# Edge counts of a graph attention layer: sorted into buckets and counted behind the projection, instead of counted one tile at a time ahead of it

## The chip, the cores and the metric

The kernel runs on one core of a Trainium2 chip, in one launch. The metric is the device time in microseconds (us) of that core. Five engines work in parallel, each through its own list of instructions, and meet at semaphores: TensorE (PE, matmuls, writes PSUM; PEld is its weight load), VectorE (DVE), ScalarE (ACT), GpSimd (POOL) and SyncE (SP, which issues the DMAs).

## The reference

```python
xn = layernorm(x)                                      # x: 625 x 1024
z  = einsum('ni,hif->nhf', xn, W)                      # 4 heads of 256: 625 x 1024
el, er = (z * a_l).sum(-1), (z * a_r).sum(-1)
e  = leaky_relu(el[src] + er[dst], 0.2)                # 10000 edges
ex = exp(e - segment_max(e, dst)[dst])
gnn = segment_sum(ex / segment_sum(ex, dst)[dst] * z[src], dst)
q, k, v = split(xn @ w_qkv); q, k = elu(q) + 1, elu(k) + 1       # 16 heads of 64
mix = (q @ (k.T @ v)) / (q @ k.sum()) @ w_o
x = x + gnn + mix
out = x + ternary_ffn(layernorm(x)) + bias             # int8 rounded input, ternary weights
```

An edge (src, dst) enters the attention only through its pair. So the kernel needs one 625 x 625 table, how many edges go from each source to each target; with it, the edge softmax becomes a dense one with the exponentials multiplied by `counts`, and with `no_edge`, a mask where the count is zero.

## The kernel before

The 625 nodes are five tiles (NT) of 125 rows (P), the 1024 features eight blocks of 128 (KT). Projections go in chunks of 512 columns: z is Z_CH = 2 chunks, then KV_CH = 4 chunks of k and v, then q, the output product and the ternary layer. A float32 product is three passes, high by high, low by high, high by low (`three_pass`, L988 to L990); ScalarE makes the high part of each weight unit (`hi_unit`, L344), GpSimd the low part (`lo_quad`, L304), four units ahead of TensorE. A `step` is one weight unit against all five row tiles, 15 matmuls of 512 columns.

Before z the edges are counted. They are 80 columns of 125 edges. For each column VectorE (`onehots`, L586 and L588) writes a one-hot of the targets, 125 x 626 in bf16, and one of the sources by pairs, 125 x 314, whose value is 1 for an even source and 4096 for an odd one. TensorE (`edge_tiles`, L1015) multiplies them, five matmuls a column, one for each tile of 125 targets, and adds up in PSUM banks 0 to 4. The 80 columns are three groups (GROUP_SEGS), so that no sum passes 4096; after each ScalarE copies the banks (`copy_counts`, L371). Between the columns VectorE does the layer norm of each row tile in steps (`statistics`), ScalarE scales the rows (`row`, L352, L355), TensorE transposes them (`row_transposes`, L1004), and ScalarE and GpSimd split them into `act_hi` and `act_lo`. ScalarE also takes the absolute sums of the ternary weights there (`abs_of`, L377).

When the last group is copied, TensorE begins z (L988, the loop over `step(c, k, ...)`), and VectorE unpacks the three packed sums into `counts` and `no_edge` (L636 to L660). VectorE's list then goes on with `take_z(0)` (`junk` L678, the products with a_l and a_r, and `z_lo` L684), the ternary scale, the diagonals (L693), `take_z(1)` and the scores. Two waits tie the engines here:

```python
act.wait_ge(z_used, c * NT + (nt + 1))        # ScalarE, ahead of each copy of z out of PSUM (L417)
dve.sem_inc(z_used, NT)                       # VectorE, behind no_edge
pe.wait_ge(bank_free, (ci + NG - 1) * NT + (nt + 1))   # TensorE, ahead of a chunk's first step
```

The next loop (j = 0, 1) runs k and v with the GAT units between the steps: in step 1 `el` is spread over the partitions (L1092), and from step 5 on (UNIT_STEPS) each unit transposes `prob` (L1078), which VectorE makes from the scores (L732), ScalarE's exponentials and `counts` (L751, L753). Everything behind it is the same in both kernels.

## Time and profile before

| | us |
|---|---|
| median of 3 runs | 469.44 (467.74 to 470.69) |
| the profiled execution, its own time | 471.35 |
| its span, first to last instruction | 469.6 |
| TensorE busy | 446.0 |
| VectorE busy | 345.0 |
| ScalarE busy | 190.5 |
| GpSimd busy | 138.4 |

The busy time of an engine is an average over stages with different limits: it tells who is full, not who is waited for. A window gives the same numbers for one stage. The chain that ended last goes back from the last instruction, at each step to what released it. A row of the timeline has the start, the length, the engine, the line in the kernel, and the tile written <- the tiles read. The granted clock is TensorE's, as a share of 2.4 GHz.

### The profile page before, as it was taken

To read this page: it belongs to the slowest core of one execution; us is meant where nothing else is said; L and a number is where in the kernel's file an instruction comes from. 1 tells how busy PE (TensorE), PEld (TensorE's weight loads), DVE (VectorE), ACT (ScalarE), POOL (GpSimd) and SP (SyncE) were. 2 spreads that over 40 slices of the span, in tenths; PEclk is the share of its full clock that TensorE was granted. 3 is DMA by queue.
4 is the path that set the end of the run, shared out by engine and by line. 5 is a ranking of instruction groups with operands and counts; after the bars stand their busy time and mean duration, and the time that the engine had idled before them with its cause. 6 is when DMAs were issued, how large, how long until landed. Compare 5 with 4: busy or idle time off the path is not lost.

```text
span 469.6 us, 8351 instructions
## 1 busy us (share of the span) xinstructions
PE 446.0 (95%) x2707; PEld 384.2 (82%) x2707; DVE 345.0 (73%) x905; ACT 190.5 (41%) x337; POOL 138.4 (29%) x105
## 2 busy tenths in 40 slices
PE   7799999989999899999999999999999999989897
PEld 4699898768787787779888788799999888868665
DVE  5999997998569778984157799636556468798773
ACT  2476562125173475445245544425433122212162
POOL 2421133544331422122232321247776000051200
PEclk9989999999999999999999999999999999998999
DMA  8833240322221311111121111136663011020024
GB/s 206 241 91 91 89 136 1 90 67 67 67 67 47 89 47 45 46 45 47 45 67 45 45 45 45 45 93 198 183 188 105 22 46 45 7 82 1 1 87 132
DMA packets 19207, 36.47 MB, mean 78 GB/s; under 512 B 2593, under 2 KB 2843, under 8 KB 19054
## 3 DMA queue, kind: packets, MB, share of 16 engines
q1 hardware_dynamic: 19179, 36.11, 26.6%
q8 instruction: 16, 0.26, 0.2%
q14 instruction: 12, 0.10, 0.1%
HBM read 33.54 MB, written 2.56 MB: 77 GB/s over the span
## 4 chain that ended last, share of the span: by engine, by line
PE 63%; DVE 22%; issue 7%; ACT 3%; DMA 2%; SPq 1%; DVEq 1%; ACTq 0%
PE ps L988 14%; PE ps L989 14%; PE ps L990 14%; PE ps L1015 9%; PE ps L1243 4%; DMA w_raw<-in_weights 2%; PE ps L1078 2%; DVE exp_a L751 2%; DVE score L732 2%; PE ps L1130 2%; DVE junk L678 1%; DVE k_sb L721 1%; DVE packed L642 1%; PE ps L1113 1%; DVE unpack L639 1%
## 5 line engine op out<-in xcount | busy, mean ns | idle before, releaser
L304 POOL TENSOR_TENSOR w_lo<-w_raw,w_hi 128x512 fp32r<-128x512 f32 x52 | 73.4, 1416 | 179.7 <-ACT w_hi L344 179.7
L988 PE MATMUL ps<-w_hi,act_hi 128*125 128x512 f32 x240 | 96.8, 403 | 2.3 <-ACT tmp L417 2.2
L989 PE MATMUL ps<-w_lo,act_hi 128*125 128x512 f32 x240 | 94.6, 394 | 0.0
L990 PE MATMUL ps<-w_hi,act_lo 128*125 128x512 f32 x240 | 94.5, 394 | 0.0
L1015 PE MATMUL ps<-onehot_src,onehot_dst 125*125 125x314 bf16 x400 | 60.2, 310 | 5.0 <-DVE onehot_src L588 4.9
L1015 PEld LDWEIGHTS ps<-onehot_src,onehot_dst 125*125 125x125 bf16 x400 | 54.9, 143 | 9.8 <-DVE onehot_src L588 5.8
L344 ACT ACTIVATE w_hi<-w_raw 128x512 fp32r<-128x512 f32 x52 | 32.8, 633 | 73.0 <-PE ps L990 70.9
L988 PEld LDWEIGHTS ps<-w_hi,act_hi 128*125 128x125 f32 x240 | 44.5, 185 | 12.8 <-ACT tmp L417 2.6
L990 PEld LDWEIGHTS ps<-w_hi,act_lo 128*125 128x125 f32 x240 | 44.5, 185 | 11.3
L989 PEld LDWEIGHTS ps<-w_lo,act_hi 128*125 128x125 f32 x240 | 44.5, 185 | 9.9
L988 PE MATMUL ps<-act_hi,w_hi 128*128 128x312 f32 (+1 forms) x128 | 39.7, 310 | 0.0
L989 PE MATMUL ps<-act_lo,w_hi 128*128 128x312 f32 (+1 forms) x128 | 39.1, 306 | 0.0
L990 PE MATMUL ps<-act_hi,w_lo 128*128 128x312 f32 (+1 forms) x128 | 39.1, 306 | 0.0
L588 DVE TENSOR_SCALAR onehot_src<-iota,src_half,src_worth 125x314 bf16<-125x314 f16 x80 | 35.8, 447 | 0.0
L988 PE MATMUL ps<-wo_hi,act_hi 128*125 128x512 f32 (+1 forms) x88 | 34.3, 389 | 0.0
L989 PE MATMUL ps<-wo_lo,act_hi 128*125 128x512 f32 (+1 forms) x88 | 33.4, 380 | 0.0
L990 PE MATMUL ps<-wo_hi,act_lo 128*125 128x512 f32 (+1 forms) x88 | 33.2, 377 | 0.0
L586 DVE TENSOR_SCALAR onehot_dst<-iota,dst_f 125x626 bf16<-125x626 f16 x80 | 32.4, 405 | 0.9 <-DVE bn L599 0.4
L337 POOL TENSOR_TENSOR x_sb<-x_sb,bias_sb 125x1024 f32<-125x1024 f32 x5 | 11.8, 2371 | 67.8 <-DMA bias_sb<-in_bias 50.9
L456 ACT ACTIVATE pt_hi<-ps 125x625 fp32r<-125x625 f32 x20 | 13.9, 693 | 36.1 <-PE ps L1078 36.1
L988 PE MATMUL ps<-z_hi,pt_hi 125*125 x100 | 28.1, 281 | 0.0
L989 PE MATMUL ps<-z_lo,pt_hi 125*125 x100 | 28.0, 280 | 0.0
(151 smaller groups left out, 878.6 us busy)
## 6 DMA issues: line engine op xcount, KB each, us to landing
w_raw<-in_weights SPq DMA_DIRECT2D x80, 256.0 KB, 2.7
f_raw<-in_ffn_weights SPq DMA_DIRECT2D x32, 256.0 KB, 2.9
x_sb<-in_x SPq DMA_DIRECT2D x5, 448.0 KB
out<-x_sb SPq DMA_DIRECT2D x9, 224.0 KB
alr<-in_a_lr SPq DMA_DIRECT2D x1, 896.0 KB
bias_sb<-in_bias SPq DMA_DIRECT2D x1, 448.0 KB
x_sb<-in_x SPq DMA_DIRECT2D x5, 52.0 KB
out<-x_sb SPq DMA_DIRECT2D x9, 26.0 KB
```

The lines of the kernel that those rows point to most:

```text
L304: pool.tensor_tensor(w_lo[:, s, :], w_raw[:, s, :], w_hi[:, s, :].bitcast(f32), ALU.subtract).then_inc(w_ready, 1)
L337: pool.tensor_tensor(x_sb[:, t, :], x_sb[:, t, :], bias_sb[:], ALU.add).then_inc(biased, 1)
L344: act.activation(w_hi[:, slot, :], w_raw[:, slot, :], ACT.Copy).then_inc(w_hi_ready, 1)
L456: act.activation(pt_hi[:], pt_ps[:P, 0:NT, :P], ACT.Copy).then_inc(pt_hi_ready, 1)
L586: dve.tensor_scalar(onehot_dst[:, s % RING, :], iota[:], dst_f[:, ds(n * SEG + s, 1)], None, ALU.is_equal).then_inc(oh_ready, 1)
L588: dve.tensor_scalar(onehot_src[:, s % RING, :], iota[:, :HALF], src_half[:, ds(n * SEG + s, 1)], src_worth[:, ds(n * SEG + s, 1)], ALU.is_ ...
L732: dve.tensor_tensor_reduce(out=score[:, u % 2, :], in0=no_edge[:, dt, :N], in1=el_rows[:, a, :], scale=1.0, scalar=2 * NEG, op0=ALU.add, o ...
L988: pe.matmul(dst, a[0], b[0], start=first, stop=False)
L989: pe.matmul(dst, a[0], b[1], start=False, stop=False)
L990: return pe.matmul(dst, a[1], b[0], start=False, stop=last)
L1015: last = pe.matmul(ps[:P, nt, :HALF], onehot_dst[:, s, nt * P:(nt + 1) * P], onehot_src[:, s, :], start=opens and s == 0, stop=False)
L1243: last = pe.matmul(ps[:P, part_bank(t, i), :hi - lo], quant_t[:, t % 2, k, :P], tern[:, k, lo:hi], start=k == 0, stop=k == KT - 1)
```

## The change

The edges are no longer counted ahead of z. They are sorted on the chip first, and counted behind z.

A bucket is one tile of 125 targets by a third of the sources (SPART = 209): 5 x 3 = 15 buckets. VectorE works out each edge's bucket (`buckets`), the running count in each bucket by a scan, and, with the totals of the rows by two small matmuls (L1166, L1167), its place (`places`). Each bucket gets whole units of 256 places, 54 units in all, that is 108 tiles of 128 slots. Ten `route` batches move the edges' codes to their places: VectorE writes one-hots of the place's partition (`route_p`) and column (`route_c`, multiplied by the code), TensorE multiplies eight columns of edges a batch (L1152) into bank 7. `decode` takes target and source back out of the code. Then 14 batches of `count_onehots` (108 tiles in eights, the last a half) give a one-hot of 125 targets and one of 209 sources, and TensorE needs one matmul of 209 columns for a tile, where it needed five of 314 for a column of edges. Which PSUM columns a unit adds to depends on its bucket: `unit_columns` writes the addresses, and TensorE loads them into registers, four at a time (`load_units`, TENSOR_LOAD, L1157). The one-hots are f16 with four tiles innermost, so TensorE reads them with a stride of four elements.

The order: `buckets` stands ahead of the layer norm; the row tiles' low halves are now VectorE's (`split_lo`) and not GpSimd's; `abs_of` moves into z's first half on ScalarE, with the DMAs of the ternary weights on SyncE between those of z's weights; route batches 0 to 7 stand behind steps 4 to 7 of z's first half, 8 and 9 behind step 0 of its second; the counting stands behind z. New waits: TensorE's matmul for the ternary scale waits for `fscale` and `slots`, its clearing of bank 7 waits for the scale (`fscale`, 2), ScalarE's `z_hi` waits for the last route batch, the j loop's first step waits for `count_out` (five copies of the counts), VectorE's `no_edge` for all eight.

```diff
+    SPART = (N + 2) // 3
+    NB = NT * 3
+    UT = 2
+    USLOTS = UT * 128
+    UNITS = (E + NB * (USLOTS - 1)) // USLOTS
+    TILES = UNITS * UT
+    ULOAD = 4
+    UPAD = (UNITS + ULOAD - 1) // ULOAD * ULOAD
+    BATCH = 8
+    NROUTE = ET // BATCH
+    NOH = (TILES + BATCH - 1) // BATCH
+    RSLOTS = 4
+    OHSLOTS = 7
+    CODE0 = 1024
...
+            for k in range(KT - 1):
+
+                sp.wait_ge(w_ready, k + 1)
+                sp.dma_start(w_raw[:, k % QUAD, :], weights[QUAD + k]).then_inc(raw_in[k % QUAD], 16)
+                for s in range(2):
+                    sp.wait_ge(f_abs, 2 * k + s + 1)
+                    sp.dma_start(f_raw[:, s, :], ffn_weights[2 * k + 2 + s]).then_inc(f_in[s], 16)
+            sp.wait_ge(w_ready, KT)
+            sp.dma_start(w_raw[:, QUAD - 1, :], weights[QUAD + KT - 1]).then_inc(raw_in[QUAD - 1], 16)
+            with sp.Fori(KT // QUAD + 1, QA) as q:
...
+                    act.activation(act_hi[:, 4 * b:4 * b + 4, t * P:(t + 1) * P], row_ps(t, b),
+                                   ACT.Copy).then_inc(act_hi_in, 1)
+
+            def abs_of(u):
+
+                act.wait_ge(f_in[u % 2], 16 * (u // 2 + 1))
+                act.activation(f_raw[:, u % 2, :], f_raw[:, u % 2, :], ACT.Abs,
+                               accum_out=abs_sum[:, u:u + 1]).then_inc(f_abs, 1)
...
-            with act.Fori(0, Z_CH) as c:
+            for c in range(Z_CH):
                 for k in range(KT - 1):
                     step_split(c, k, c * 2 + (k // QUAD + 1))
+                    if c == 0:
+                        abs_of(2 * k)
+                        abs_of(2 * k + 1)
                 for nt in range(NT):
                     act.wait_ge(proj_done, c * NT + (nt + 1))
 
                     act.wait_ge(z_used, c * NT + (nt + 1))
                     act.activation(tmp[:, nt, :], ps[:P, nt, :], ACT.Copy).then_inc(bank_free, 1)
                 step_split(c, KT - 1, c * 2 + 2)
+                if c == 0:
+                    abs_of(NU - 2)
+                    abs_of(NU - 1)
+                    act.wait_ge(route_used, NROUTE)
                 for nt in range(NT):
-                    act.wait_ge(bank_free, (c + NG) * NT + (nt + 1))
-                    act.activation(z_hi[:, nt, ds(c * CH, CH)], tmp[:, nt, :], ACT.Copy).then_inc(z_hi_ready, 1)
+                    act.wait_ge(bank_free, c * NT + (nt + 1))
+                    act.activation(z_hi[:, nt, c * CH:(c + 1) * CH], tmp[:, nt, :], ACT.Copy).then_inc(z_hi_ready, 1)
+
+
+            act.wait_ge(count_done, 8)
...
+                dve.tensor_tensor(member.rearrange("p (b e) -> p b e", e=ET), bucket_iota[:],
+                                  edge_c.rearrange("p (o e) -> p o e", o=1).broadcast_to([P, NB, ET]),
+                                  ALU.is_equal).then_inc(edge, 1)
+                dve.wait_ge(edge, 10)
+
+                dve.tensor_tensor_scan(upto[:, 1:], member[:], member[:], 0.0, ALU.add, ALU.max).then_inc(edge, 1)
+                dve.wait_ge(edge, 11)
+                dve.tensor_tensor(row_tot[:], upto[:, ET::ET], upto[:, 0:NB * ET:ET], ALU.subtract).then_inc(masks, 1)
...
+            def route_onehots(i):
+
+                slot = i % RSLOTS
+                if i >= RSLOTS:
+                    dve.wait_ge(route_used, i - RSLOTS + 1)
+
+                def of(t, n):
+                    return t[:, BATCH * i:BATCH * (i + 1)].rearrange("p (g o t) -> p g o t", o=1, t=4).broadcast_to([P, 2, n, 4])
+
+                def counted(n):
+                    return count_iota[:P, :n, :].rearrange("p (o n) t -> p o n t", o=1).broadcast_to([P, 2, n, 4])
+
+                dve.tensor_tensor(route_p[:, slot], counted(128), of(edge_p, 128), ALU.is_equal).then_inc(routes, 1)
+                dve.tensor_tensor(route_c[:, slot], counted(TILES), of(edge_c, TILES), ALU.is_equal).then_inc(routes, 1)
+                dve.wait_ge(routes, 3 * i + 2)
+                dve.tensor_tensor(route_c[:, slot], route_c[:, slot], of(edge_v.bitcast(f16), TILES), ALU.mult).then_inc(routes, 1)
...
+            def count_onehots(i):
...
+                dve.tensor_tensor(onehot_d[slot][:, :g], counted(P), of(slot_d, P), ALU.is_equal).then_inc(oh_ready, 1)
+                dve.tensor_tensor(onehot_s[slot][:, :g], counted(SPART), of(slot_s, SPART), ALU.is_equal).then_inc(oh_ready, 1)
...
+            buckets()
+            statistics(0)
+            statistics(1)
+            root(0)
+            statistics(2)
+            root(1)
+            split_lo(0)
+            for t in range(1, NT):
+                if t + 2 < NT:
+                    statistics(t + 2)
+                if t + 1 < NT:
+                    root(t + 1)
+                split_lo(t)
+            codes()
+            places()
+            unit_columns()
             dve.wait_ge(row_t, 2 * NT)
-
-
-            ups = 0
-            dve.wait_ge(bank_free, NG * NT)
-            for g in range(NG):
-                pk, un, cs = packed[:, g, :, :], unpack[:], csum[:]
-                dve.tensor_scalar(un, pk, -BASE / 2.0 + 48.0, 1.0 / BASE, ALU.add, ALU.mult).then_inc(up, 1)
-                ups += 1
-                dve.wait_ge(up, ups)
-                dve.tensor_scalar(un, un, MAGIC, MAGIC, ALU.add, ALU.subtract).then_inc(up, 1)
-                ups += 1
-                dve.wait_ge(up, ups)
-                dve.scalar_tensor_tensor(pk, un, -float(BASE), pk, ALU.mult, ALU.add).then_inc(up, 1)
-                if g == 0:
-                    dve.tensor_copy(cs, un).then_inc(up, 1)
-                elif g < NG - 1:
-                    dve.tensor_tensor(cs, cs, un, ALU.add).then_inc(up, 1)
-                else:
-                    dve.tensor_tensor(counts[:, :, 1:NPAD:2], cs[:, :, :NPAD // 2], un[:, :, :NPAD // 2],
-                                      ALU.add).then_inc(up, 1)
-                ups += 2
-                dve.wait_ge(up, ups)
-            for g in range(1, NG - 1):
-                dve.tensor_tensor(packed[:, 0, :, :], packed[:, 0, :, :], packed[:, g, :, :], ALU.add).then_inc(up, 1)
-                ups += 1
-                dve.wait_ge(up, ups)
-            dve.tensor_tensor(counts[:, :, 0:NPAD:2], packed[:, 0, :, :NPAD // 2],
-                              packed[:, NG - 1, :, :NPAD // 2], ALU.add).then_inc(up, 1)
-            ups += 1
-            dve.wait_ge(up, ups)
-            dve.tensor_scalar(no_edge[:], counts[:], 0.0, NEG, ALU.is_equal, ALU.mult).then_inc(up, 1)
-            ups += 1
-            dve.wait_ge(up, ups)
             dve.sem_inc(z_used, NT)
-
-
-            dve.wait_ge(alr_in, 2 * 16)
-            dve.sem_inc(el, 1)
+            dve.wait_ge(edge, 15)
+            for i in range(NROUTE):
+                route_onehots(i)
+            decode()
...
+            OH_A = OHSLOTS // 2
+            for i in range(OH_A):
+                count_onehots(i)
+            dve.wait_ge(alr_in, 2 * 16)
+            dve.sem_inc(el, 1)
             take_z(0)
-
-            dve.wait_ge(fs_ps, 1)
-            dve.tensor_scalar(scales[:, 0:1], ps[:, 7, 0:1], 1.0 / (D * D), None, ALU.mult).then_inc(fscale, 1)
+            dve.wait_ge(f_abs, NU)
+            dve.reduce_sum(abs_sum[:, NU:NU + 1], abs_sum[:, :NU], axis=AX.X).then_inc(fscale, 1)
+            for i in range(OH_A, OHSLOTS):
+                count_onehots(i)
+            scale_of()
             diagonals(0)
-            dve.wait_ge(fscale, 2)
-            dve.tensor_scalar(scales[:, 1:2], scales[:, 0:1], 0.5, None, ALU.mult).then_inc(fscale, 1)
-            dve.tensor_scalar(scales[:, 2:3], scales[:, 0:1], -0.5, None, ALU.mult).then_inc(fscale, 1)
-            dve.wait_ge(fscale, 4)
+            for i in range(OHSLOTS, NOH):
+                count_onehots(i)
             take_z(1)
             dve.wait_ge(z_used, (1 + Z_CH) * NT)
             diagonals(1)
+            dve.wait_ge(count_out, 8)
+            dve.tensor_scalar(no_edge[:], counts[:], 0.0, NEG, ALU.is_equal, ALU.mult).then_inc(up, 1)
...
+            for k in range(KT):
+                step(0, k, k + 1, k % QUAD)
+                if k >= 4:
+                    route(2 * (k - 4))
+                    route(2 * (k - 4) + 1)
+
+            unit_at = []
+            for k in range(KT):
+                step(1, k, KT + k + 1, k % QUAD)
+                if k == 0:
+                    route(NROUTE - 2)
+                    route(NROUTE - 1)
+                    pe.wait_ge(cols_ready, 1)
+                elif k == KT - 2:
+                    pe.wait_ge(fscale, 1)
+                    pe.wait_ge(slots, 1)
+                    pe.matmul(ps[:, 7, 0:1], ones[:], abs_sum[:, NU:NU + 1], start=True, stop=True).then_inc(fs_ps, 1)
+                unit_at += load_units(k)
+
+            flat = ps[:P].rearrange("p b n -> p (b n)")
+            for b in (5, 6, 7, 0, 1, 2, 3, 4):
+                if b == 7:
+                    pe.wait_ge(fscale, 2)
+                elif b < NT:
+                    pe.wait_ge(bank_free, NT + b + 1)
+                pe.matmul(ps[:P, b, :2 * SPART], zeros[:, :P], zeros[:, :2 * SPART], start=True, stop=False)
+            for u in range(UNITS):
+                if u % ULOAD == 0 and u // ULOAD >= KT:
+                    unit_at += load_units(u // ULOAD)
+                for i in range(u * UT, (u + 1) * UT):
+                    if i % BATCH == 0:
+                        pe.wait_ge(oh_ready, 2 * (i // BATCH) + 2)
+                    slot, g, t = i // BATCH % OHSLOTS, i % BATCH // 4, i % 4
+                    last = pe.matmul(flat[:, ds(unit_at[u], SPART)], onehot_d[slot][:, g, :, t], onehot_s[slot][:, g, :, t],
+                                     start=False, stop=False)
+                    if i % BATCH == BATCH - 1:
+                        last.then_inc(oh_used, 1)
+                unit_at[u] = None
+            for b in range(8):
+                pe.matmul(ps[:P, b, :2], zeros[:, :P], zeros[:, :2], start=False, stop=True).then_inc(count_done, 1)
 
```

VectorE's list between the two halves of z, before. `junk` and `z_lo` are `take_z`, `scales` the ternary scale:

```order
L678 SCALAR_TENSOR_TENSOR junk,elr<-tmp,alr 125x256 x3
L684 TENSOR_TENSOR z_lo<-tmp,z_hi 125x512 [waits z_hi_ready,el]
L700 TENSOR_SCALAR scales<-ps 128x1 [waits fs_ps]
L693 TENSOR_TENSOR diag<-ident,elr 125x625 x2
L703 TENSOR_SCALAR scales<-scales 128x1 [waits fscale]
L704 TENSOR_SCALAR scales<-scales 128x1
L678 SCALAR_TENSOR_TENSOR junk,elr<-tmp,alr 125x256 [waits el,bank_free,fscale]
L678 SCALAR_TENSOR_TENSOR junk,elr<-tmp,alr 125x256 x3
```

The same place now; `onehot_d_NN` and `onehot_s_NN` are slots of the count's one-hots:

```order
L742 TENSOR_TENSOR onehot_d_85<-count_iota,slot_d 128x1000
L743 TENSOR_TENSOR onehot_s_92<-count_iota,slot_s 128x1672
L742 TENSOR_TENSOR onehot_d_86<-count_iota,slot_d 128x1000
L743 TENSOR_TENSOR onehot_s_93<-count_iota,slot_s 128x1672
L822 TENSOR_SCALAR scales<-ps 128x1 [waits fs_ps]
L824 TENSOR_SCALAR scales<-scales 128x1 [waits fscale]
L825 TENSOR_SCALAR scales<-scales 128x1
L816 TENSOR_TENSOR diag<-ident,elr 125x625 [waits fscale]
L816 TENSOR_TENSOR diag<-ident,elr 125x625
L742 TENSOR_TENSOR onehot_d_80<-count_iota,slot_d 128x1000 [waits oh_used]
L743 TENSOR_TENSOR onehot_s_87<-count_iota,slot_s 128x1672
```

Between the scale and the second `take_z` stand seven batches of one-hots that wait for TensorE (`oh_used`), and the scale stands behind the four batches ahead of it.

TensorE's list where z starts, before:

```order
L1015 MATMUL ps<-onehot_src,onehot_dst 125x314 [waits oh_ready]
L1015 MATMUL ps<-onehot_src,onehot_dst 125x314 x4
L1038 MATMUL ps<-zeros 125x2 x5
L1058 MATMUL ps<-abs_sum,ones 128x1 [waits fscale,act_ready]
L1061 UNCONDITIONAL_BRANCH
L1061 ISA
L1047 ISA [waits w_ready]
L988 MATMUL ps<-w_hi,act_hi 125x512 [waits bank_free]
L989 MATMUL ps<-w_lo,act_hi 125x512
```

And where z ends now:

```order
L1128 MATMUL ps<-w_hi,act_lo 125x512
L1157 TENSOR_LOAD unit_col
L1214 MATMUL ps<-zeros 125x418 x2
L1214 MATMUL ps<-zeros 125x418 [waits fscale]
L1214 MATMUL ps<-zeros 125x418 [waits bank_free] x5
L1222 ISA [waits oh_ready]
L1222 MATMUL ps<-onehot_s_87,onehot_d_80 125x209 x2
L1222 ISA
```

What stood ahead of z, with L1015, stands behind it, with L1222; the ISA rows work out a unit's PSUM address, and the third clearing waits for VectorE's scale.

## Rows read from the trace of the kernel before

**Rows 1.** The page: the chain that ended last, shares by engine and line.
```profile
PE 63%; DVE 22%; issue 7%; ACT 3%; DMA 2%; SPq 1%; DVEq 1%; ACTq 0%
```

**Rows 2.** Windows: busy us (instructions) per engine, granted clock, DMA share, GB/s.
```profile
0.00:74.70 74.70, 68.31 (x464) 62.59 (x464) 66.44 (x211) 39.42 (x84) 20.54 (x24) 0.98 0.47 134
74.70:104.90 30.20, 28.09 (x120) 22.13 (x120) 27.72 (x15) 6.28 (x13) 12.56 (x7) 1.00 0.23 61
104.90:132.80 27.90, 27.85 (x120) 22.29 (x121) 18.66 (x57) 11.60 (x21) 10.69 (x8) 1.00 0.24 66
```

**Rows 3.** The page, costliest groups: busy us, mean ns, idle before.
```profile
L1015 PE MATMUL ps<-onehot_src,onehot_dst 125*125 125x314 bf16 x400 | 60.2, 310 | 5.0 <-DVE onehot_src L588 4.9
...
L588 DVE TENSOR_SCALAR onehot_src<-iota,src_half,src_worth 125x314 bf16<-125x314 f16 x80 | 35.8, 447 | 0.0
```

**Rows 4.** The chain in order of time, 100 to 110 us.
```profile
103.17 0.99 DVE no_edge L660
...
104.95 0.50 PE ps L988
```

**Rows 5.** The chain in order of time, 150 to 156 us.
```profile
152.36 1.76 DVE prob L753
...
154.18 0.81 PE ps L1078 x5
```

**Rows 6.** Groups of VectorE, 0 to 133 us.
```profile
L642 DVE SCALAR_TENSOR_TENSOR packed<-unpack,packed 125x1570 f32<-125x1570 f32 x3 | 5.4, 1795 | 0.1
...
L636 DVE TENSOR_SCALAR unpack<-packed 125x1570 f32<-125x1570 f32 x3 | 2.9, 980 | 3.3 <-ACT packed L371 3.2
...
L660 DVE TENSOR_SCALAR no_edge<-counts 125x3130 bf16<-125x3130 int16 x1 | 1.0, 979 | 0.0
...
L578 DVE TENSOR_SCALAR src_worth<-half_i 125x80 f32<-125x80 int32 x1 | 0.2, 193 | 0.0
```

**Rows 7.** Timeline of ScalarE, first tiles: start, length.
```profile
9.67 1.13 ACT L352 ACTIVATE rows<-x_sb,ln 125x1024 f32<-125x1024 f32 x1
...
24.75 0.59 ACT L363 ACTIVATE act_hi<-ps 128x500 fp32r<-128x500 f32 x1
```

**Rows 8.** The longest pieces of the whole chain; eight transposes at two clocks.
```profile
23.88 1.67 PE ps L1004 x8
...
36.70 0.91 PE ps L1004 x8
```

**Rows 9.** Window 20 to 24 us; the granted clock stands before the DMA share.
```profile
20.00:24.00 4.00, 3.18 (x17) 2.69 (x18) 3.87 (x13) 1.57 (x2) 1.06 (x1) 0.81 0.26 64
```

**Rows 10.** Timeline of VectorE, 75 to 165 us.
```profile
104.93 0.43 DVE L678 SCALAR_TENSOR_TENSOR junk<-tmp,alr 125x256 f32<-125x256 f32 x1 [0.78 <-ACT tmp L417]
...
110.70 1.69 DVE L684 TENSOR_TENSOR z_lo<-tmp,z_hi 125x512 fp32r<-125x512 f32 x1
...
113.01 1.50 DVE L678 SCALAR_TENSOR_TENSOR junk<-tmp,alr 125x256 f32<-125x256 f32 x1
...
114.90 0.69 DVE L684 TENSOR_TENSOR z_lo<-tmp,z_hi 125x512 fp32r<-125x512 f32 x1
...
121.79 0.15 DVE L700 TENSOR_SCALAR scales<-ps 128x1 f32<-128x1 f32 x1
...
146.80 1.53 DVE L693 TENSOR_TENSOR diag<-ident,elr 125x625 f32<-125x625 f32 x2
```

**Rows 11.** Timeline of GpSimd, 110 to 122 us.
```profile
110.56 1.29 POOL L304 TENSOR_TENSOR w_lo<-w_raw,w_hi 128x512 fp32r<-128x512 f32 x1 [1.82 <-ACT w_hi L344]
```

**Rows 12.** Timeline of TensorE: two-column matmuls, and the el matmuls.
```profile
60.90 0.40 PE L1038 MATMUL ps<-zeros 125*125 125x2 f16 x5
...
139.83 2.35 PE L1092 MATMUL ps<-diag,ones 125*125 125x125 f32 x20
```

**Rows 13.** VectorE sequencer at line 588: ns min/median/max, first and last start.
```profile
L588 DVEq FUSED_REGOPS  x48: 46/46/46, 22.5 to 58.2; - x48
```

**Rows 14.** The page, DMA issues: KB each, us to landing.
```profile
w_raw<-in_weights SPq DMA_DIRECT2D x80, 256.0 KB, 2.7
```

381 lines of the change are left out of this document (218 added, 163 removed).

## The prediction

> **What bounds the kernel now.** I read the page first. TensorE has 63% of the chain that ended last, VectorE 22% [rows 1]. Such shares hide the stage that the change touches, so I asked for windows with their edges at the program's own joints [rows 2]: to 74.7 us the edges are counted; to 104.9 TensorE multiplies z's first half, and VectorE is just as full (27.7 of 30.2 us) with something else, the unpacking of the counts; to 132.8 z's second half. The costliest groups say what fills the first window: 400 one-hot matmuls (60.2 us), and on VectorE twice 80 one-hots, the dearer kind 0.45 us each [rows 3]. The chain in order of time shows who ends it: VectorE's counts and mask end at 104.16, and only then can ScalarE copy z, and TensorE goes on at 104.95 [rows 4] (it is idle for 30.20 - 28.09 = 2.1 us of that window [rows 2]). Last, the chain at 154 shows VectorE's prob releasing the transposes L1078 [rows 5]. From there on the two programs are the same. So the question is one date: when do the first L1078 transposes start, at 154.2 now? After it 469.6 - 154.2 = 315.4 us remain.
>
> **Removed.** All of the first window but the normalised rows, and the 15 unpacking instructions, which are beside z's first half and cost the path only those 2.1 us.
>
> **The rows first (A).** z needs all five row tiles. Edges land at 3.55 us. VectorE then has ten small bucket instructions (0.19 us as L578, 0.23 with its wait [rows 6]: 2.3), `member` with 1200 elements and the scan with 1200. Rows bound them: one-source f32 takes 0.98 us for 1570 elements (2 a cycle), two-source f32 1.80 (1 a cycle), one-source 16-bit 0.98 for 3130 (4 a cycle) [rows 6]. `member` is two-source 16-bit and I give it 2 a cycle, 0.8; the scan feeds its sum back, between 1 a cycle (1.4) and half that (2.7), I take 2.7. Statistics of tile 0 end at 3.55 + 5.8 + 1.7 = 11.0. ScalarE is then the long engine: per tile a square root 0.1, shift and scale 1.05 each from start to start (1.13 long), 0.3 between them and two copies of 0.5 (0.59 long), 3.5 us [rows 7], five times 17.6, four weight splits 2.5, some 2.9 of waiting for transposes, which run at half clock after an idle TensorE (1.67 for eight against 0.91 [rows 8], granted clock 0.81 in 20 to 24 us [rows 9]). Then the last low part: 35.0 us.
>
> **VectorE's chain (B).** From 35 on I follow VectorE, since TensorE's own work (8 + 8 steps of 15 matmuls, 27.9 us for 120 [rows 2], and the routes) would end z at 98. 24 instructions of codes, places and unit columns: 3 x 1.43, 2 x 1.05 and 19 x 0.23, 10.7 us: 45.7.
> A route batch is 1024 + 864 + 864 elements, all 16-bit, two-source. No row has this kind. The ends: at 1 a cycle as the f32 rows, 3.2 us; at 2, 1.75 us (0.16 + n / (2 x 0.96), less the 0.08 by which the next starts early, the last one waiting). The rows show that halving the element's size doubles the one-source rate [rows 6], so I take 1.75: ten are 17.5. A count batch has 1000 + 1672: 1.55 us, or 2.95; 13.5 of them.
> Holds: a GpSimd weight split of 1.3 us keeps a two-source VectorE instruction waiting: z_lo is 1.69 instead of 0.69 at 110.70 and junk 1.50 instead of 0.43 at 113.01 [rows 10], the first beside the GpSimd row at 110.56 [rows 11]. All new VectorE work is of the held kind, and GpSimd has one split per z step. I count six in the routes (7.8), one in the first and one in the second group of count batches (2.6).
> The sum: 45.7 + 17.5 + 7.8 = 71.0; last route batch on TensorE 0.8 and five decode instructions 1.4: 73.2; three count batches and a hold 5.9: 79.1; take_z(0) 15.3 (104.93 to 121.79 less a wait of 1.6, its holds inside [rows 10]): 94.4; the reduction 0.3, four batches and a hold 7.5: 102.2. Only now comes the scale, and TensorE waits for it before it clears bank 7: z ended near 99, a stall of about 3. Scale and two diagonals (1.5 for both [rows 10]) 2.5: 104.7. The other 6.5 batches, each needing a slot back from TensorE, 10.1: 114.8.
>
> **TensorE and ScalarE behind it (C).** A count matmul has 125 weight columns and 209 moving ones. The long ones of 314 take 0.15 (60.2 for 400 [rows 3]), those of 2 columns at about 0.06 (0.40 for five with the last's latency [rows 12]); I take 0.10, 0.8 a batch, so VectorE at 1.55 sets the pace and TensorE ends the last half batch and the eight closers 1.1 us later: 115.9. ScalarE's five copies of 418 columns, 0.45 each: 118.2; behind `count_out` the whole of the k and v loop stands. Then five steps (17.4) and the el matmuls (2.35 with the last one's tail [rows 12], some 2.1 in a row): 137.7. VectorE's side meets it: 114.8 + take_z(1) 13.9 + mask 1.0 + 7.3 from the diagonals to prob (146.80 to 154.12 [rows 5, 10]) = 137.0.
> Two small terms are left. TENSOR_LOAD, 14 on TensorE's queue. Rows bound one between a register operation (0.046 [rows 13]) and a DMA's landing (2.7 [rows 14]); I take 0.1, as it asks four words of on-chip memory: 1.4. And 0.9 for z's first steps at half clock. Date: 140.0, a gain of 14.2. 471.35 - 14.2 = 457.2 for a profiled execution; the median of the runs shown is 1.9 below the profiled one: **455**.
> The Trainium skill (DMA: Bandwidth & Descriptors, "Latency and other measured facts") gives tensor_load a floor of about 600 ns; no row shows one. By it eight in z's second half would add 4.8, of which the 3 us stall covers most, and six between count batches would hide under VectorE: an estimate of 457.
>
> Why so little, when 74.7 - 35 = 40 us are won at the front? TensorE's new work is only some 21 us, but VectorE's 65 us of sorting and one-hots stand partly behind z and serially with take_z.
>
> **Rivals.**
> 1. *One element a cycle (slower).* If two-source 16-bit instructions with stride-0 rows run as the f32 two-source rows do, routes cost 1.43 more each (14.3) and count batches 1.39 (18.8): 33 us on the chain, date 173, **488**. It decides from 43% of that loss on. For: every two-source row of this trace is at 1 a cycle, and the fours inside the broadcast are short. Against: 16-bit one-source rows double. 0.12. The Trainium skill (Vector Engine (DVE) Microarchitecture Reference, "Performance modes") has two 16-bit values per read if every operand is 16-bit with inner step 1, a row read again and again included, but a single element read again at 1 a cycle; no run here shows it. By the first 455 stands, by the second 488; the inner four make it the first.
> 2. *TensorE reads the one-hots slowly.* They are taken with a stride of four elements, which no row has. At the rate of the f32 transposes (0.91 / 8 / 125, 0.9 ns a column [rows 8]) a count matmul takes 0.19: from 103.3 on 20.5 us, date 148.7, **464**. A half clock in the gaps of this stage gives the same. 0.14.
> 3. *TENSOR_LOAD stalls.* At 1.3 us each: 8 x 1.3 less the 2.5 of the stall, and 6 x 0.55 above VectorE's pace, 11 us: **466**. At the upper end, 2.7, even 486. 0.10.
> 4. *No holds.* GpSimd's splits fall into VectorE's small gaps: 10.4 us less on VectorE, of which TensorE's own work lets 8 through: **447**. 0.07. Against: the rows above show them collide now.
> 5. *The change does nothing:* the counts are off z's path already but for 2.1 us, which speaks for it; the 40 us in front speak against. 0.02.
>
> **How the numbers follow.** The forecast has 0.55, with 449 to 461 as its own range (two holds more or less 2.6, scan and statistics 1.5, loads 3). With rivals 4 below and 2 and 3 above, 447 to 471 leaves out rival 1 and the ends of 3, some 0.17. A measurement of this kernel tells about 1% (4.7 us) from nothing. Faster by more: 0.55 + 0.07 + most of rival 2, 0.73. Within: 0.12. Slower: rival 1 and the end of 3, 0.15.
>
> **What would show it.** Right: z's first full step near 36 us; route batches 1.75 us apart where GpSimd rests and about 3 where it splits; TensorE waiting some 3 us for the scale before bank 7; seven count batches at VectorE's 1.55; the first L1078-like transposes near 140, and the rest 315 us long as before. Wrong: a 1024-element one-hot at 1.2 us instead of 0.7 (rival 1); count matmuls 0.15 us or more apart inside a batch (2); gaps behind each TENSOR_LOAD (3); a stretch after the date that differs by more than 2 us, which I have not priced.

## The result, and the profile after

The changed kernel takes 478.82 us (median of 4 runs, 478.39 to 481.45) beside 470.06 us of the kernel before in the same session: a ratio of 1.0207, interval 1.0166 to 1.0247. The whole interval lies above 1: the change makes the kernel slower, by about 2%. The forecast was 455 us, and 478.82 lies outside its range of 447 to 471.

The prediction turned on one date, the first `prob` transposes: 154.2 us before [rows 5], 140.0 forecast. TensorE's instructions of that line after (ns min/median/max, first and last start):

```profile
L1243 PE MATMUL ps<-ident,prob x100: 268/272/373, 164.4 to 312.2; 125*125 125x125 f32 x100
```

The first start is 164.4: 24.4 later than forecast, 10.2 later than before. I call it the date of a run. What follows it takes 476.7 - 164.4 = 312.3 us (315.4 before; the last section says where such a difference comes from). Together that is the miss of the profiled execution: 478.53 measured, 457.2 forecast, and 24.4 - 3.1 = 21.3. So it went wrong ahead of that date. The windows of core 0 with the edges at the joints of the new program answer to [rows 2]: rows, z's first half, a gap, z's second half without its last step, that step, counting, and the way to the transposes.

```profile
core 0: us, PE busy (x) PEld busy (x) DVE busy (x) ACT busy (x) POOL busy (x), PEclk, DMA share, GB/s
0.00:36.00 36.00, 13.57 (x51) 10.13 (x52) 24.69 (x67) 19.84 (x30) 10.67 (x17) 1.00 0.55 153
36.00:71.10 35.10, 35.10 (x183) 28.30 (x181) 32.27 (x55) 9.52 (x26) 7.78 (x5) 1.00 0.36 113
71.10:79.40 8.30, 0.05 (x2) 0.04 (x1) 0.00 (x0) 4.13 (x12) 2.53 (x2) 0.59 0.32 99
79.40:107.00 27.60, 27.60 (x121) 21.95 (x121) 20.36 (x47) 10.05 (x20) 10.74 (x7) 0.94 0.36 113
107.00:118.80 11.80, 8.34 (x27) 6.41 (x27) 11.51 (x24) 4.27 (x8) 1.58 (x2) 0.71 0.17 45
118.80:139.80 21.00, 21.00 (x117) 20.88 (x115) 19.18 (x55) 2.46 (x5) 1.23 (x1) 1.00 0.04 13
139.80:164.40 24.60, 22.13 (x97) 18.02 (x97) 9.95 (x26) 9.72 (x17) 5.72 (x4) 0.86 0.13 33
```

The rows are ready when I said. Then come three things that the forecast does not have: a gap of 8.3 us in which TensorE and VectorE both do nothing, a last step of z stretched over 11.8 us, and 21 us of counting. The waits of TensorE from 60 to 150 us name the places (waiting instruction, releaser, us in total, times, longest):

```profile
PE ps L1126 <- ACT tmp L438: 8.3, 1, 8.3
PE ps L1205 <- DVE abs_sum L835: 3.5, 1, 3.5
PE ps L1126 <- ACT counts L451: 2.5, 1, 2.5
```

**The gap at 71.** TensorE stands for ScalarE's copies `tmp`, which free the banks of z's first half. Such a line names only the last link; the chain in order of time shows what ScalarE itself stood for (start us, us, what):

```profile
64.53 1.55 POOL w_lo L345
66.08 4.78 DMA w_raw<-in_weights
...
71.42 1.33 ACT f_raw L402 x4
72.77 0.33 SPq L295
73.14 3.75 DMA w_raw<-in_weights
77.45 1.32 ACT f_raw L402 x4
78.77 0.49 ACT tmp L438
```

Here `w_raw` is a weight unit as loaded, `w_hi` its high part, and `f_raw` a unit of the ternary (FFN) weights, of which ScalarE takes the absolute sum, |w|. It is a loop: weight unit, |w| of two FFN units, weight unit. Two turns of it, first in SyncE's list of DMA issues, then in ScalarE's (each row ends with the idle time before it and its releaser):

```profile
47.73 0.94 SPq L295 DMA_DIRECT2D f_raw<-in_ffn_weights  x2
48.72 0.43 SPq L292 DMA_DIRECT2D w_raw<-in_weights  x1
53.52 0.94 SPq L295 DMA_DIRECT2D f_raw<-in_ffn_weights  x2
54.51 0.43 SPq L292 DMA_DIRECT2D w_raw<-in_weights  x1
```
```profile
52.25 0.63 ACT L378 ACTIVATE w_hi<-w_raw 128x512 fp32r<-128x512 f32 x1 [3.93 <-DMA w_raw<-in_weights]
52.79 0.61 ACT L402 ACTIVATE f_raw<-f_raw 128x512 f32<-128x512 f32 x1
...
58.02 0.63 ACT L378 ACTIVATE w_hi<-w_raw 128x512 fp32r<-128x512 f32 x1 [3.91 <-DMA w_raw<-in_weights]
```

SyncE's list is in order. A weight unit stands behind the two FFN loads before it, these wait until ScalarE has taken |w| of the last two, and in ScalarE's list that |w| stands behind the high part of the last weight unit. So only one weight unit is ever under way, and a turn takes 58.02 - 52.25 = 5.8 us (the last two, from one w_hi to the next, 7.1 and 6.0: the unit issued at 66.08 took 4.78 to land, and no row says why), while TensorE uses a unit every 5.1 where routes are multiplied and every 3.5 where not. The units in hand run out, and the copies of z stand in ScalarE's list behind the seventh turn. VectorE waits too, 16.7 us, since its decode needs the last two route batches, and these stand on TensorE behind the first step of z's second half.

**The last step of z.** TensorE waits 3.5 us for the sum of |w|, which VectorE takes only behind take_z(0), and does most of that step at half its clock: 13 of the 15 matmuls start 0.43 us or more apart and not 0.23 (granted clock 0.71 in the window above, 0.56 from 111 to 117.8 us).

**Counting.** The matmuls of L1222, and those of the routes, L1152:

```profile
L1222 PEld LDWEIGHTS ps<-onehot_s,onehot_d x108: 191/193/198, 118.6 to 138.8; 128*125 128x125 f16 x108
L1222 PE MATMUL ps<-onehot_s,onehot_d x108: 354/369/374, 118.8 to 139.0; 128*125 128x209 f16 x108
```
```profile
L1152 PEld LDWEIGHTS ps<-route_c,route_p x80: 113/117/137, 54.0 to 85.9; 125*128 125x128 f16 x80
```

The durations hold latency; the pace is in the starts: (139.0 - 118.8) / 107 = 0.19 us. VectorE's batches (0.68 + 1.02, 1.53 from start to start) are ready before TensorE wants them.

### The profile page after: what moved, and what is told of

Read it like the earlier page. It is cut to its first block, busy times and chain, and to the rows that moved or that the text cites. A ratio compares the mean times of both kernels' runs of the same rounds, so it can differ in the third digit from the quotient of the medians.

```text
span 476.7 us, 7532 instructions
## 1 busy us (share of the span) xinstructions
PE 428.1 (90%) x2498; PEld 365.5 (77%) x2498; DVE 329.5 (69%) x835; ACT 182.7 (38%) x320; POOL 128.3 (27%) x98
## 3 DMA queue, kind: packets, MB, share of 16 engines
q1 hardware_dynamic: 19179, 36.11, 25.5%
## 4 chain that ended last, share of the span: by engine, by line
PE 62%; issue 16%; DVE 13%; ACT 3%; POOL 3%; DMA 2%; DVEq 0%; POOLq 0%; ACTq 0%; SPq 0%
PE ps L1126 15%; PE ps L1127 15%; PE ps L1128 15%; PE ps L1222 4%; PE ps L1411 4%; DVE junk L801 3%; POOL w_lo L345 2%; PE ps L1243 2%; PE ps L1298 2%; DMA w_raw<-in_weights 2%; DVE exp_a L889 2%; DVE score L870 2%; DVE k_sb L859 1%; PE ps L1281 1%; ACT k_sb L470 1%
## 5 line engine op out<-in xcount | busy, mean ns | idle before, releaser
L1126 PE MATMUL ps<-w_hi,act_hi 128*125 128x512 f32 x240 | 101.0, 421 | 10.8 <-ACT tmp L438 8.3
L1127 PE MATMUL ps<-w_lo,act_hi 128*125 128x512 f32 x240 | 97.9, 408 | 0.0
L1128 PE MATMUL ps<-w_hi,act_lo 128*125 128x512 f32 x240 | 97.4, 406 | 0.0
L1126 PEld LDWEIGHTS ps<-w_hi,act_hi 128*125 128x125 f32 x240 | 46.8, 195 | 21.7 <-POOL w_lo L345 8.5
L1128 PEld LDWEIGHTS ps<-w_hi,act_lo 128*125 128x125 f32 x240 | 46.5, 194 | 12.1
L1127 PEld LDWEIGHTS ps<-w_lo,act_hi 128*125 128x125 f32 x240 | 46.7, 195 | 10.3
L371 POOL TENSOR_TENSOR x_sb<-x_sb,bias_sb 125x1024 f32<-125x1024 f32 x5 | 11.8, 2387 | 64.0 <-DMA bias_sb<-in_bias 51.1
L899 DVE TENSOR_TENSOR pt_lo<-ps,pt_hi 125x625 fp32r<-125x625 f32 x20 | 16.2, 808 | 17.3 <-ACT pt_hi L491 16.6
L1128 PE MATMUL ps<-z_hi,pt_lo 125*125 x100 | 28.0, 280 | 0.0
L891 DVE CUSTOM_DVE_ANT_0 prob<-exp_a,counts 125x625 f32<-125x625 f32 x20 | 24.0, 1201 | 0.7
L359 POOL TENSOR_TENSOR wo_lo<-w_raw,wo_hi 128x512 fp32r<-128x512 f32 x16 | 22.7, 1422 | 6.6 <-ACT wo_hi L512 6.6
```

The costliest lines, as they stand in the source:

```text
L359: pool.tensor_tensor(wo_lo[:, k, c * CH:(c + 1) * CH], w_raw[:, stream_o(i) % QUAD, :], wo_hi[:, k, c * CH:(c + 1) * CH].bitcast(f32), ALU ...
L891: dve.tensor_tensor_reduce(out=prob[:, u % 2, :], in0=exp_a[:], in1=counts[:, dt, :N], scale=1.0, scalar=0.0, op0=ALU.mult, op1=ALU.add, a ...
L899: dve.tensor_tensor(pt_lo[:], pt_ps[:P, 0:NT, :P], pt_hi[:].bitcast(f32), ALU.subtract).then_inc(pt_ready, 1)
L1126: pe.matmul(dst, a[0], b[0], start=first, stop=False)
L1127: pe.matmul(dst, a[0], b[1], start=False, stop=False)
L1128: return pe.matmul(dst, a[1], b[0], start=False, stop=last)
```

## The experiments

I state every result by its date, the start of the first transposes in its one profile, and by the ratio to the kernel before, where there are several runs (a2, a3, b2 and e3 have one). A date is good to about 1 us: from the last count matmul to the date TensorE's program is the same in the changed kernel and all its runs but e1 and e4, and that stretch is 24.2 to 25.5 us. Three causes: (T1) the loop of loads, (T2) the slow count matmul, (T3) the place of the scale. "On the changed kernel" holds for all.

**a1_loads_ahead.**

```diff
+            LEAD = 3
+            for k in range(LEAD):
+                sp.wait_ge(w_ready, k + 1)
+                sp.dma_start(w_raw[:, k % QUAD, :], weights[QUAD + k]).then_inc(raw_in[k % QUAD], 16)
             for k in range(KT - 1):
-                sp.wait_ge(w_ready, k + 1)
-                sp.dma_start(w_raw[:, k % QUAD, :], weights[QUAD + k]).then_inc(raw_in[k % QUAD], 16)
+                if LEAD + k < KT:
+                    sp.wait_ge(w_ready, LEAD + k + 1)
+                    sp.dma_start(w_raw[:, (LEAD + k) % QUAD, :], weights[QUAD + LEAD + k])\
+                      .then_inc(raw_in[(LEAD + k) % QUAD], 16)
```

> One edit: SyncE issues z's weight units three units ahead of the FFN units, instead of each one behind the two FFN units before it. Theory 1 (z's first half starves because a weight unit is asked for only when ScalarE has taken |w| of two FFN units that were themselves behind the last weight unit; period 5.8 us against the 5.1 to 5.3 that a TensorE step with two route batches needs, and the copies of z stand behind it): the 8.25 us wait of TensorE at 71 and the half clock behind it (1.7) go, the second half of z starts near 71.5 instead of 79.4, VectorE decodes the slots near 72 instead of 86.3, and as take_z(0) then ends near 94, the 3.5 us wait for the FFN scale (and its half clock, 2.6) goes too. First prob transposes near 149 (164.4), time about 463, ratio to before 0.985. Rival (the stall is VectorE's or the DMA queues': x rows, weights and FFN units only swap their waiting): w_hi still waits for w_raw some 4 us per unit, transposes within 3 us of 164, ratio 1.01 to 1.02. Counting itself stays at 0.19 us a matmul by both.

Date 154.8 (9.6 earlier), 469.34 us, ratio 1.0004 (0.996 to 1.0048). The gap is gone, and no w_hi waits for a DMA from 44 us on:

```profile
44.20 0.63 ACT L381 ACTIVATE w_hi<-w_raw 128x512 fp32r<-128x512 f32 x1 [1.68 <-PE ps L1131]
47.66 0.63 ACT L381 ACTIVATE w_hi<-w_raw 128x512 fp32r<-128x512 f32 x1 [0.71 <-PE ps L1131]
```

T1 is shown. The second half of my expectation was wrong: the wait for the scale stays (3.4 us). The last route batches stand behind a step of z's second half, so decode, take_z(0) and the sum all moved with z, by 9.7 us; nothing between them closed.

**e3_lead_one**, the same with `LEAD = 1`:

> a1_loads_ahead with the weight units only one ahead of the FFN units instead of three, on the changed kernel. If the cause is that weight unit and FFN pair formed one serial loop (5.8 us a turn), one unit ahead breaks it: the loop of FFN pairs alone takes DMA 2.7, hi 0.6, |w| 1.3 and the issues, under 5.1, so the second half of z starts within 1 us of a1's 71.5 and the transposes are near 155. If it is rather the bytes that must arrive per step, one unit ahead regains only part: start at 74 to 78.

Date 154.1 (one run of 473.48 us, whose stretch behind the date is a long one, 317.5); the route batches ahead of z's second half at 70.96 us, 1.3 later than in a1. The same bytes come in the same order but for one place, and 10.3 us go: the order was the cause, not the volume.

**a2_moving_packed, a3_weights_packed, a4_inner_two.** The operands' views, and the layout:

```diff
# a2: moving operand
-  onehot_s[slot][:, g, :, t]
+  onehot_s[slot][:, g].rearrange("p n t -> p (n t)")[:, SPART * t:SPART * (t + 1)]
# a3: weights
-  onehot_d[slot][:, g, :, t]
+  onehot_d[slot][:, g].rearrange("p n t -> p (n t)")[:, P * t:P * (t + 1)]
# a4: TI = 2 tiles side by side, in route_*, onehot_* and count_iota
-  [128, 2, SPART, 4]
+  [128, BATCH // TI, SPART, TI]
```

> Only the view of the moving operand of the count matmuls is changed: 209 neighbouring elements of the same one-hot tile instead of every fourth one, so the counts are no longer the counts (which edges are masked changes), all instructions and their number stay. If the stride of the MOVING operand is what makes a count matmul cost 0.19 us: 0.09 to 0.11 us each, PE then waits for VectorE's batches (1.53 us per 8), the 108 take about 12 us instead of 20.5 and the time is some 8 us under after's. If it is the weights' stride, the register address, or the operands' number of rows: 0.19 us stays, 20.5 us.

> The counterpart: only the view of the WEIGHTS of the count matmuls (125 neighbouring elements instead of every fourth), moving operand as it was; again the counts are not the counts. Moving theory: 0.19 us each stays (20.5 us for 108). Weight theory: LDWEIGHTS 0.19 falls to about 0.13 or less and the 108 take 12 to 14 us. For the moving theory speaks that the route matmuls, also strided by four in both operands but with 108 moving columns, take 0.095 each.

> Routes and counts laid out with two tiles side by side instead of four (stride of 4 bytes instead of 8), everything else as it was. If TensorE's cost comes with how many elements it finds next to each other: count matmuls at 0.10 to 0.13 us, 108 in about 12 us (VectorE's pace of 1.53 per 8 then sets it), gain about 8 us on after: ratio to before near 1.003. If any stride costs the same: 0.19, ratio 1.02. VectorE's side is a risk of its own: if its two-a-cycle rate needs the inner four, its one-hots go from 0.68/1.02 to 1.1/1.8 us, routes and counting get slower and the ratio is above 1.04.

The weight loads of the count matmuls in a2, a3 and a4, in this order (an LDWEIGHTS row, since matmuls overlap and weight loads of a burst follow each other):

```profile
L1222 PEld LDWEIGHTS ps<-onehot_s,onehot_d x108: 192/213/217, 119.5 to 132.1; 128*125 128x125 f16 x108
```
```profile
L1222 PEld LDWEIGHTS ps<-onehot_s,onehot_d x108: 137/155/156, 117.8 to 137.9; 128*125 128x125 f16 x108
```
```profile
L1223 PEld LDWEIGHTS ps<-onehot_s,onehot_d x108: 136/138/143, 115.9 to 128.2; 128*125 128x125 f16 x108
```

First to last start: 12.6, 20.1, 12.3 us, against 20.2 unedited. A packed moving operand alone brings 0.117 us a matmul; packed weights alone bring nothing, though each load is shorter (155 ns and not 193): the moving side still sets 0.19. a4 halves the stride on both sides, and on VectorE nothing changes (1.02 us a `onehot_s`). TensorE's burst in a4, then VectorE's pace:

```profile
116.10 7.83 PE L1223 MATMUL ps<-onehot_s,onehot_d 128*125 128x209 f16 x80
124.08 0.98 PE L1223 MATMUL ps<-onehot_s,onehot_d 128*125 128x209 f16 x8 [0.16 <-DVE onehot_s L744]
```

7.83 / 80 = 0.098 us. Date 152.7 (a4; 156.4 in a2, 163.6 in a3), and a4's ratio 0.9986 (0.9952 to 1.002). T2 is shown. a4's route matmuls, 16 in 0.96 us (1.78 before the edit), run at twice the pace too; the gap at 71 is 10.5 us there instead of 8.3, since TensorE comes to it earlier.

**b2_fixed_place**: a4 with `ps[:P, u % 8, :SPART]` for `flat[:, ds(unit_at[u], SPART)]` and no `load_units`.

> a4_inner_two with the count matmuls at fixed PSUM addresses and without the 14 TENSOR_LOADs: the counts land in the wrong places, all other work is the same. If loads and register addresses cost TensorE what I priced (1.4) or nothing: the steps of z's second half stay at 3.49 us, the count matmuls inside a burst at 0.095 to 0.098, transposes within 1.5 us of a4's 152.7. If they cost the 0.6 us each that the Trainium skill's DMA page gives: 4 us or more earlier.

Date 153.6, so no gain (a4: 152.7). A stretch says it more closely: from the start of z's second half to TensorE's wait for the sum of |w| stand six of the loads, and it takes 27.06 us with them (a4, 78.33 to 105.39) and 26.97 without (b2, 79.35 to 106.32). Six loads cost TensorE 0.1 us at most there, and the 108 count matmuls go from first to last start in 12.2 us in both. In the changed kernel a TENSOR_LOAD is on the queue for 0.33 us:

```profile
L1157 PEldq TENSOR_LOAD <-unit_col x14: 327/331/529, 84.1 to 135.1; - x14
```

**b1_scale_first.**

```diff
+            dve.wait_ge(f_abs, NU)
+            dve.reduce_sum(...).then_inc(fscale, 1)
             for i in range(OH_A):
                 count_onehots(i)
...
             take_z(0)
-            dve.wait_ge(f_abs, NU)
-            dve.reduce_sum(...).then_inc(fscale, 1)
+            scale_of()
             for i in range(OH_A, OHSLOTS):
                 count_onehots(i)
-            scale_of()
```

> On the changed kernel, one edit on VectorE: the sum of |w| is taken before the first count batches (all 16 parts are there by 85 us), and the scale right behind take_z(0), before four count batches. Theory (TensorE stood for VectorE's order, not for its work): the 3.5 us wait of the scale's matmul before z's last step goes, and with it the half clock of that step (2.6), nothing takes its place since the first three batches are ready and counting runs at TensorE's 0.19: counting ends near 133.3 instead of 139.4, transposes near 158.3, ratio 1.007. Rival (the clock does not fall because of that wait, or the batches come late instead): gain of 3 us or less, ratio 1.014 to 1.02.

In the profile it is as the theory has it: the wait is gone, the last step of z, from 107 us, runs at full clock, and the date is 157.4, 7.0 earlier. Its window:

```profile
100.00:110.00 10.00, 10.00 (x46) 8.01 (x45) 9.86 (x30) 3.70 (x6) 4.39 (x3) 1.00 0.27 81
```

The timed ratio is 1.0139 (1.009 to 1.0187), less of a gain than the date has, and 1.007 lies outside. This interval overlaps that of the changed kernel (1.0166 to 1.0247), so T3 rests on the trace. The profiled run took 471.40 us, the other three 474.62 to 476.78; the last section has what varies behind the date, but with one trace I can't show that it is this.

**c2_all_three, d1_routes_early, e2_diag_late.** c2 joins a1, a4 and b1. d1 adds to it:

```diff
+            route(NROUTE - 2)
+            route(NROUTE - 1)
             for k in range(KT):
                 step(1, k, KT + k + 1, k % QUAD)
                 if k == 0:
-                    route(NROUTE - 2)
-                    route(NROUTE - 1)
...
-            diagonals(0)
             for i in range(OHSLOTS, NOH):
                 count_onehots(i)
+            diagonals(0)
```

and e2 adds only the second of its two edits.

> Weight units ahead, inner two and scale first together, on the changed kernel. If the three causes are all there is: the second half of z from 70.5 to 99, VectorE's take_z(0) ends near 98.5, counting is then at VectorE's pace of 1.53 us a batch and ends near 117.5, transposes near 142, time about 458, ratio 0.974 (the sum of the three gains, 9.6 + 10.5 + 6, would give 142.7 less what they share). If the gains are not additive because VectorE becomes the bound from the decode on: transposes at 146 to 148, ratio 0.984.

> c2_all_three, and two moves that shorten VectorE's chain if that is now the bound: the last two route batches are multiplied before the first step of z's second half and not behind it (VectorE's decode 3.5 us earlier), and the two diagonals are written behind the last count batch (1.5 us). If VectorE's chain decode, three batches, take_z(0), eleven batches sets the end of counting: it ends 4 to 5 us before that of c2_all_three, ratio lower by 0.009 to 0.010, about 0.965. If TensorE or the start of z's second half sets it: no more than 1 us.

> c2_all_three with the two diagonals (1.5 us on VectorE) behind the last count batch. Of d1_routes_early's two moves this is the one that I still hold for right; the other cost TensorE waits of 2.1 and 1.2 us and a half clock at the head of z's second half. If VectorE's batches set the end of counting: it ends 1.5 us before c2's 118.4 (the 2.0 us wait of TensorE inside counting goes), date 142.1, ratio 0.971. If not: 143.6, 0.975.

c2: date 143.6 (1.6 later than I gave), 457.42 us, ratio 0.9747 (0.9703 to 0.9792), as expected. e2: date 142.2, ratio 0.971 (0.9649 to 0.9772), as expected. d1: date 145.9, ratio 0.9863 (0.982 to 0.9906), a clear miss. Its TensorE:

```profile
72.41 0.56 PE L1156 MATMUL ps<-route_c,route_p 125*128 125x108 f16 x8 [2.14 <-DVE route_c L718]
74.17 0.90 PE L1156 MATMUL ps<-route_c,route_p 125*128 125x108 f16 x8 [1.20 <-DVE route_c L718]
74.85 0.77 PE L1130 MATMUL ps<-w_hi,act_hi 128*125 128x512 f32 x1
75.42 0.63 PE L1131 MATMUL ps<-w_lo,act_hi 128*125 128x512 f32 x1
```

I had moved two matmul groups ahead to save VectorE 3.5 us, and put them in front of work that was ready. TensorE waits 3.3 us for them, then does most of a step of z at half clock; z's second half starts at 74.9 instead of 69.6. There was nothing to save either: VectorE writes the last route batch until 74.1, and its decode starts at 75.1, in c2 at 74.4. The step of z that stood ahead of them was not in their way, it was cover.

**e1_busy_in_wait, e4_best.** e1 on c2:

```diff
+            for _ in range(32):
+                last = pe.matmul(ps[:P, 7, 2 * SPART:], zeros[:, :P], zeros[:, :512 - 2 * SPART], start=True, stop=True)
+            last.then_inc(count_done, 1)
```

> c2_all_three, and 32 matmuls of zeros into the unused columns of bank 7 while TensorE waits 2.5 us for ScalarE's copies of the counts (ScalarE's last copy waits for them). Theory (TensorE's first step after a wait runs at the lower clock because TensorE did nothing before it): the 12 or 13 matmuls that start 0.43 us apart behind that wait start 0.23 apart, the windows from 120 to 130 show a granted clock of 1.0, transposes 2.6 us earlier than c2's 143.6, near 141.0, ratio 0.969. Rival (the clock falls for what the count matmuls before it did, or with the time): the half clock stays, date 143 to 144, ratio 0.975.

> c2_all_three with both e1's and e2's edit. If both hold they add: date 139.5, ratio 0.966. If counting is at VectorE's pace either way and the clock stays: 0.971 to 0.975.

The first matmuls behind the wait for the counts, in c2 and then in e1:

```profile
121.42 0.79 PE L1130 MATMUL ps<-w_hi,act_hi 128*125 128x512 f32 x1 [2.47 <-ACT counts L455]
122.00 0.63 PE L1131 MATMUL ps<-w_lo,act_hi 128*125 128x512 f32 x1
122.43 0.63 PE L1132 MATMUL ps<-w_hi,act_lo 128*125 128x512 f32 x1
```
```profile
118.34 2.04 PE L1238 MATMUL ps<-zeros 125*125 125x94 f16 x32
120.94 0.49 PE L1132 MATMUL ps<-w_hi,act_hi 128*125 128x512 f32 x1 [0.56 <-ACT counts L455]
121.28 0.39 PE L1133 MATMUL ps<-w_lo,act_hi 128*125 128x512 f32 x1
121.50 0.40 PE L1134 MATMUL ps<-w_hi,act_lo 128*125 128x512 f32 x1
```

From 0.43 to 0.23 us apart; date 140.6, ratio 0.9704 (0.964 to 0.9768). Of the 3.0 us between the dates 0.5 lie ahead of the edit (the last count matmul starts at 117.8 and not 118.3), 2.5 behind it. The time from the end of counting to the next step is the same within 0.2 us: only what TensorE did in it differs. The ratios of c2, e1 and e2 alone can't be told apart, their intervals overlap; the traces can.

e4 has both edits: date 139.2, 454.13 us (452.57 to 458.03), ratio 0.9683 (0.9629 to 0.9737). It beats both kernels. Its windows of z's first half, second half, counting, copies and the way to the transposes, beside those of the changed kernel above:

```profile
36.00:69.20 33.20, 32.62 (x185) 25.54 (x183) 32.11 (x52) 17.67 (x42) 10.84 (x7) 1.00 0.49 151
69.20:98.50 29.30, 29.29 (x142) 23.22 (x140) 28.18 (x66) 10.72 (x21) 12.19 (x8) 1.00 0.27 83
98.50:117.00 18.50, 14.22 (x127) 12.03 (x125) 18.47 (x24) 3.81 (x8) 1.41 (x1) 1.00 0.10 28
117.00:119.50 2.50, 1.96 (x33) 1.83 (x32) 2.46 (x11) 2.41 (x7) 0.00 (x0) 1.00 0.00 0
119.50:139.20 19.70, 19.68 (x96) 16.25 (x97) 18.31 (x57) 7.21 (x12) 5.55 (x4) 1.00 0.10 29
```

In counting VectorE is busy 18.47 of 18.50 us: there it is the bound now, as the forecast had it.

## Why the prediction was wrong

**A, rows ready at 35.0.** Right within 1.6 us: the last low part ends at 36.6. `member` takes 0.78 us (0.8), the scan 2.66 (2.7). z's matmuls start at 34.9, the first eight at half clock.

**B, VectorE's chain.** Its prices were right: route batches follow 1.76 us apart where nothing holds them (1.75), a count batch takes 1.53 (1.55), take_z(0) 16.0 (15.3). That the routes also end when I said, 69.6 (71.0), is partly luck, two errors of opposite sign: they begin 3.0 late (48.7 for 45.7), and I counted six holds of 1.3 in them (7.8), where there are three of 0.7 to 1.1 (2.8), since the starved loop brings GpSimd a split only every 5.8 us. In e4, where the loop does not starve, there are five of about 1.1. Rival 1 is refuted: 1000 elements of two-source 16-bit in 0.68 us. Rival 4, no holds, is refuted by the same rows.

**The step that failed** is the sentence "From 35 on I follow VectorE, since TensorE's own work ... would end z at 98". It takes for granted that TensorE finds its weights. I counted the splits of GpSimd only as a hold on VectorE, and never followed a weight unit from SyncE's issue through ScalarE to TensorE, though the diff puts 16 |w| units from the row stage into z's first half, each pair tied to a weight load. [rows 14] had the 2.7 us of landing; 2.7, the high part 0.6, two |w| 1.3 and the issues about 1 add up to 5.6, more than a step. That sum could have been made from the rows of before. It comes out near the 5.8 partly by luck: in the trace the unit takes 3.5 to land (54.51 to 58.02), and a part of |w| and of the issues runs side by side. The loop cost 8.3 us of standing and 1.7 of half clock: 9.6 by a1.

**The scale.** "A stall of about 3" was the right size (3.5) at the wrong place. I had it before bank 7; TensorE's list has it before the last step of z, so that most of a step then ran at half clock, which I had not priced (2.6). Wait and half clock are 6.1; b1 has 7.0 by the date.

**C, the count matmul.** 0.10 taken, 0.19 measured: rival 2's figure to the digit. In the choice I went by the length of packed rows and took the stride as a mere doubt, though [rows 8] was the one row near it. But rival 2 took its rate from float32 transposes, and no run ties their 0.9 ns a column to a stride: that it fits to the digit is luck. Cost: 20.5 us of counting in place of VectorE's pace (12.3 in a4); with the routes 11.7 by the date. Rival 2 said 464 by itself; it came with the other two.

**ScalarE's copies, the half clock behind them, TENSOR_LOAD.** The copies of the five banks are 2.16 us (2.3 forecast). The half clock behind the wait for them, 2.5 by e1, was not in the sum at all: its 0.9 stood for z's first steps. TENSOR_LOAD costs nothing that b2 shows, not 1.4; rival 3 falls. The Trainium skill (DMA: Bandwidth & Descriptors, "Latency and other measured facts") has about 600 ns for one; the rows have 0.33.

**The sum again.** Counting started 15.5 us later than forecast (118.8, 103.3), took 8.4 more (21.0, 12.6), and the way from its end to the transposes took 2.8 more (24.6, against 137.7 - 115.9 = 21.8). That is 26.7; the sum had another 2.3 at its end (loads and z's first steps), which belong ahead of counting, and 26.7 - 2.3 = 24.4. So 21.6 of the 24.4 us lie ahead of counting's end, and the 2.8 behind it are mostly the half clock (2.5). The three edits together gain 20.8 (c2), less than 9.6 + 11.7 + 7.0: with them VectorE's chain is the bound, as e2 shows, which takes 1.5 us off that chain alone and moves the date by 1.4.

With e1 and e2 as well the date is 139.2, the forecast one 140.0, and the time 454 us, forecast 455. That is less of a proof than it looks: e4 has an order of VectorE's list and a filled wait that the forecast knew nothing of, and no stall for the scale, which it did have (3). What holds is the kind: the forecast was that of a kernel in which only VectorE limits; the one at hand had three limits outside it. My chances show the same fault: all the "slower" side hung on two prices of instructions, none on an order.

## What to carry to other kernels

Where a change moves instructions, follow each stream that feeds the busiest engine (issue, landing, conversion) for one whole turn and compare the turn with the rate of use: a wait in an in-order list joins streams that have nothing to do with each other. A summary of waits names the last link; read the chain behind it. And moving work earlier on an engine helps only if it is ready: what then stands behind it pays the wait and the lower clock.
